# Expert weights of a routed layer: up weights tile by tile in a ring of three, down weights of all experts held on chip

## What is computed

```python
def _L0_ffn_ref(tgt, Wr, br, W1, b1, W2, b2, gamma, beta):
    B, S, D, F, E = (2, 512, 256, 1024, 8)
    ...
    logits = jnp.einsum('bsd,ed->bse', tgt, Wr) + br
    top_v, top_i = jax.lax.top_k(logits, 2)
    top_w = jax.nn.softmax(top_v, axis=-1)
    ...
    h = jnp.einsum('bsd,efd->bsef', tgt, W1) + b1
    h = jax.nn.relu(h)
    o = jnp.einsum('bsef,edf->bsed', h, W2) + b2
    tgt2 = jnp.einsum('bsed,bse->bsd', o, router_w)
    return _layer_norm(tgt + tgt2, gamma, beta)
```

## Time and profile before

| what | us |
|---|---|
| median of 3 runs | 1827.38 |
| lowest and highest of them | 1818.76, 1833.07 |
| the profiled execution, its own time | 1823.52 |
| span of the profile | 1821.8 |
| the expert loop, from the first load of `xs` to the last output on DVE | 1156.5 to 1449.9 |

### The profile page before, as it was taken

One profiled execution on the slowest core, in us unless ns is written; L12 is line 12 of the kernel. 1 busy time (PEld: TensorE's weight loads), 2 busy tenths in 40 slices (PEclk: granted clock), 3 DMA queues, 4 the chain that ended last, 5 costly groups with the idle time before them and its releaser, 6 DMA issues.

```text
span 1821.8 us, 44029 instructions
## 1 busy us (share of the span) xinstructions
PE 1562.2 (86%) x18034; PEld 1282.3 (70%) x18034; DVE 1237.7 (68%) x2503; ACT 705.7 (39%) x1312; POOL 898.0 (49%) x862
## 2 busy tenths in 40 slices
PE   1899999999998999999999973499989855898798
PEld 0677777787777777877787752488888743566587
DVE  8757777777777678777777765244478666555765
ACT  1434544454444444444444431244534514222122
POOL 3246555665563365566565651576555616221322
PEclk9999999999999999999999986799999965655699
DMA  9134433442432253335334301799999781700001
GB/s 215 37 72 114 105 83 94 106 117 75 102 93 63 69 123 77 95 94 127 90 85 106 102 36 54 289 407 406 402 385 397 267 156 12 116 3 1 35 12 35
DMA packets 92973, 239.39 MB, mean 131 GB/s; under 512 B 17611, under 2 KB 40707, under 8 KB 92388
## 3 DMA queue, kind: packets, MB, share of 16 engines
q1 hardware_dynamic: 89028, 226.32, 43.0%
q0 software_dynamic: 3744, 10.26, 1.5%
HBM read 144.31 MB, written 39.72 MB: 101 GB/s over the span
## 4 chain that ended last, share of the span: by engine, by line
PE 53%; DVE 15%; DMA 13%; POOL 8%; issue 5%; ACT 2%; SPq 0%; DVEq 0%; ACTq 0%; POOLq 0%
PE ps L1916 21%; PE ps L2015 9%; DMA xs<-xslots 8%; PE ps L1949 5%; PE ps L1995 5%; PE ps L1996 5%; DMA latf<-wexp 4%; POOL PR L864 3%; DVE PR L1415 3%; POOL wst L876 2%; PE ps L2182 2%; DVE mxs L1349 2%; PE ps L2274 2%; DMA QS<-NM 1%; DVE wtmp L1443 1%
## 5 line engine op out<-in xcount | busy, mean ns | idle before, releaser
L864 POOL TENSOR_TENSOR PR<-PT 128x512 f16<-128x512 f32 (+1 forms) x416 | 441.2, 1070 | 421.7 <-ACT PT L1088 421.0
L1088 ACT ACTIVATE PT<-ps 128x512 f32<-128x512 f32 (+1 forms) x576 | 323.8, 596 | 366.0 <-PE ps L1996 365.8
L2015 PE MATMUL ps<-V_h,PT 128*128 128x65 f16 (+1 forms) x2304 | 324.9, 197 | 26.5 <-DVE PR L1415 20.7
L2015 PE MATMUL ps<-V_l,PT 128*128 128x65 f16 (+1 forms) x2304 | 320.4, 195 | 0.0
L2015 PE MATMUL ps<-V_l,PR 128*128 128x65 f16 (+1 forms) x2304 | 318.7, 194 | 0.0
L2015 PE MATMUL ps<-V_h,PR 128*128 128x65 f16 (+1 forms) x2304 | 318.2, 194 | 0.0
L2015 PEld LDWEIGHTS ps<-V_h,PT 128*128 128x128 bf16 (+1 forms) x2304 | 226.9, 98 | 121.2 <-issue 48.6
L1349 DVE TENSOR_REDUCE mxs<-ps 128x1 f32<-128x736 f32 x256 | 235.3, 919 | 48.3 <-PE ps L1949 48.3
L1995 PE MATMUL ps<-QA,KA 128*128 128x512 f32 (+1 forms) x576 | 247.8, 430 | 5.8 <-DMA QB<-maxT 5.2
L1996 PE MATMUL ps<-QB,KB 65*128 65x512 f32 (+1 forms) x576 | 231.0, 401 | 0.0
L2015 PEld LDWEIGHTS ps<-V_l,PT 128*128 128x128 bf16 (+1 forms) x2304 | 228.9, 99 | 0.7
(11 more groups left out here) (351 smaller groups left out, 3645.6 us busy)
## 6 DMA issues: line engine op xcount, KB each, us to landing
wx<-wsplit SPq DMA_DIRECT2D x46, 2048.0 KB, 11.4
QA<-Q_h SPq DMA_DIRECT2D x64, 256.0 KB, 4.6
latf<-wexp SPq DMA_DIRECT2D x32, 512.0 KB, 4.3
wsplit<-wst SPq DMA_DIRECT2D x32, 512.0 KB, 2.9
KA<-K_h SPq DMA_DIRECT2D x32, 275.5 KB, 3.1
KA<-K_l SPq DMA_DIRECT2D x32, 275.5 KB, 4.0
KB<-K_h SPq DMA_DIRECT2D x32, 275.5 KB, 5.4
QB<-Q_l SPq DMA_DIRECT2D x32, 256.0 KB, 5.5
```

Source lines behind the costliest of these rows:

```text
L864: nc.gpsimd.tensor_tensor(PR[0:m, s % RING, :], PT[0:m, s % RING, :], upper(s)[0:m], ALU.subtract).then_inc(s_rem_pool, 1)
L1088: nc.scalar.activation(PT[0:m, s % RING, :], score_banks[s % 2][0:m], ACT.Exp, scale=HD ** -0.5).then_inc(s_exp, 1)
L2015: mm = nc.tensor.matmul(pv_bank[:, q, :], p, v, start=(kt == 0 and q == 0 and k == 0), stop=(kt == KT - 1 and k == 3), skip_group_check=True)
```

## The change

`wx`, a ring of four with the whole expert (64 KB in each partition), is gone. In its place are `wup`, a ring of three with the up weights of a tile (24 KB in each partition), and `wdn`, which holds the down weights of all eight experts (64 KB in each partition).

- SP issues eight transfers of 1 MB for `wdn` once the last piece of `wsplit` is stored (`s_wst`), before it waits for the sorted slots (`s_sorted`). In the loop it transfers 1 MB for each tile, after a wait for the up product of tile j-3.
- PE reads the expert number of each tile itself (`value_load` in `slot_turn`). Its down matmuls address `wdn` by a register.
- Before its first down product PE waits for all of `wdn`.

```diff
@@ in the SP program
             sp.wait_ge(s_wst, 16 * E0 * PIECES)
+            for e in range(E0):
+                sp.dma_start(wdn[:, e].rearrange("p s k n -> p s (k n)"),
+                             wsplit[e, NC:].rearrange("s p k n -> p s (k n)")).then_inc(s_wdn, 16)
             sp.wait_ge(s_sorted, 3)
 
             def load_weights(j):
                 e = nc.sync.value_load(etu[0:1, j:j + 1], min_val=0, max_val=E0 - 1)
                 if j >= WR:
-                    sp.wait_ge(s_down, j - WR + 1)
-                sp.dma_start(wx[:, j % WR].rearrange("p s k n -> p s (k n)"),
-                             wsplit[bass.ds(e, 1)].rearrange("o s p k n -> p (o s) (k n)")).then_inc(s_wx[j % WR], 16)
+                    sp.wait_ge(s_up, 2 * (j - WR + 1))
+                sp.dma_start(wup[:, j % WR].rearrange("p s k n -> p s (k n)"),
+                             wsplit[bass.ds(e, 1), 0:NC].rearrange("o s p k n -> p (o s) (k n)")).then_inc(s_wup[j % WR], 16)
@@ in the PE program
             def slot_turn(j):
+                experts[j] = nc.tensor.value_load(etu[0:1, j:j + 1], min_val=0, max_val=E0 - 1)
                 pe.wait_ge(s_xs[j % XS], 16 * (j // XS + 1))
...
+            def up_weights(j, c, part, cols):
+                return wup[:, j % WR, c, "hl".index(part), cols]
+
+            def down_weights(j, piece, part, cols):
+                return wdn[:, bass.ds(experts[j], 1), piece, "hl".index(part), cols].squeeze(1)
...
             def down(j):
+                if j == 0:
+                    pe.wait_ge(s_wdn, 16 * E0)
```

More of the change, by code:

```diff
@@ L58 @@
 XS = 3
-WR = 4
+WR = 3
 DS = 6
@@ L202, in program @@
         b2s = sb1("b2s", [P, E0, D])
-        wx = sb1("wx", [P, WR, PIECES, 2, PW], F16)
+        wup = sb1("wup", [P, WR, NC, 2, PW], F16)
+        wdn = sb1("wdn", [P, E0, PIECES - NC, 2, PW], F16)
         LT0 = sb1("LT0", [E0, GR, HALF])
@@ L337, in program @@
         s_scales = sem("scales_ready")
-        s_wx = [sem(f"tile_weights{r}_loaded") for r in range(WR)]
+        s_wup = [sem(f"tile_up_weights{r}_loaded") for r in range(WR)]
+        s_wdn = sem("down_weights_loaded")
         s_b1 = sem("expert_biases_loaded")
@@ L2157, in slot_turn @@
                 mm.then_inc(s_xt, 1)
-            def weights(j, piece, part, cols):
-                return wx[:, j % WR, piece, "hl".index(part), cols]
+            def up_weights(j, c, part, cols):
+                return wup[:, j % WR, c, "hl".index(part), cols]
+            def down_weights(j, piece, part, cols):
+                return wdn[:, bass.ds(experts[j], 1), piece, "hl".index(part), cols].squeeze(1)
             def up(j):
                 pe.wait_ge(s_xl, j + 1)
-                pe.wait_ge(s_wx[j % WR], 16 * (j // WR + 1))
+                pe.wait_ge(s_wup[j % WR], 16 * (j // WR + 1))
                 for f in range(FC):
@@ L2169, in up @@
                     mm = product(hidden_banks[n % 4][:, f % 4 * P:f % 4 * P + P],
-                                 [(weights(j, c, a, slice(f * P, f * P + P)), xsp[b][:, j % 2, c, :])
+                                 [(up_weights(j, c, a, slice(f * P, f * P + P)), xsp[b][:, j % 2, c, :])
                                   for c in range(NC) for a, b in RANDL])
@@ L2182, in down @@
                         mm = nc.tensor.matmul(out_banks[j % 2], hs[a][:, j % 2, f * P:f * P + P],
-                                              weights(j, NC + f // 4, b, slice(f % 4 * D, f % 4 * D + D)),
+                                              down_weights(j, f // 4, b, slice(f % 4 * D, f % 4 * D + D)),
                                               start=(f == 0 and i == 0), stop=(f == FC - 1 and i == 2))
```

## The result

The changed kernel takes 1810.45 us (median of 8 runs, 1808.67 to 1816.01), the kernel before 1827.1 us (median of 8, 1818.76 to 1835.01). The ratio is 0.991, with a 95% interval of 0.9886 to 0.9933: 0.9% faster, 16.65 us between the medians.

A forecast was written before the change was run, and what follows sets the result against it. Bytes bound the loop's first half, above a 5.5 us tile floor. Savings of 13.6, 1.5 and 3.0 us sum to 18.1, less 1 for register steps: 17 off 1827.4 gives 1810 us, range 1799 to 1836.

The forecast's parts named there:

- the start: Around the first tiles: with half the bytes ahead, tile 3's rows land earlier; 1.5 us saved, between 0 and 3.
- the register steps: PE's expert-number read and address steps in each tile mostly fit under its array work; 1 us cost for the loop.
- Bytes bound the first stretch: Loop's first half, 1170.4 to 1327.5: DMA engines always busy at 404 GB/s, so transfers set the 6.04 us a tile.
- Tiles 1 to 27: Early loop: 26 tiles go from 6.04 to the 5.52 us floor; 13.6 us saved.
- `og`: Tile 27 to 28: DVE's 4.57 us wait for expert outputs goes; 3.0 us saved, at most 4.6.
- Later tiles: Other tiles with extra DVE work, and the last ones from 1412 on, keep their pace; nothing saved.
- `wdn`: Eight down-weight loads before the loop hide behind the router; cost 0, up to 21 us without cover.
- The rule of the Trainium skill: PE's down product: firmware-handled matmuls cost about 62 ns each; if so, 0.1 to 0.5 us in each of 35 tiles.
- DMA share near 0.6: Sign expected in the loop of the profile after the change.
- the first two (read or queue on the path): PE: read exposed, 1825 (0.20, shared with transfers not binding); or queue becomes the bound, about 1860 (slower, 0.15).
- the third (a bigger gain): Early tiles at 5.48 us, full 4.6 us on expert outputs, 3 us at the start: 22 us saved, 1805; chance 0.10.
- the fourth (the transfers don't bind): Loop stays at 6 us, set by DVE, ACT and POOL: 1827; chance 0.20, shared with the exposed PE read.

The follow-up runs named there:

- experiments 2 and 3: 2: changed kernel, but all 2 MB transferred per tile, 1828.28 us; 3: kernel before, but only the 1 MB up half transferred, 1812.47 us.
- Experiment 4: Changed kernel, but the eight down-weight transfers issued only once the tokens are scattered, so nothing covers them; 1833.79 us, ratio 1.0038.
- experiment 1: Changed kernel, but PE reads no expert number and takes down weights from a fixed place (output wrong); 1807.45 us, ratio 0.9886.
- experiments 5 and 6: Changed kernel, but PE reads the expert number twice per tile, 1812.69 us, or four times, 1861.42 us.
- experiment 8: Changed kernel with DVE's extra output work cut into nine parts per group and its expert-number read moved ahead of the part; 1798.65 us, ratio 0.9848.

## Why the prediction was right

The forecast was 1810 us, measured are 1810.45. The mechanism held. That the numbers lie only 0.45 us apart is luck: the start was taken too large by 1.5 us and the register steps by 0.6, which cancel in part, and the runs of one kernel scatter by several us. By its own steps:

- **Bytes bound the first stretch.** Shown by experiments 2 and 3: the bytes put back alone take the whole gain away, the bytes halved alone give it.
- **Tiles 1 to 27: 13.6 us.** Measured 157.1 - 144.0 = 13.1. The floor was 5.54 us and not 5.52.
- **The start: 1.5 us, between 0 and 3.** This term is wrong, and the runs show nothing in its place: from the bias load `b2s` (1096.05 and 1101.58) to the first `hf` the kernels take 68.0 and 68.1 us (0.3 us less from the first load of `xs` on, 0.4 us more up to it), and tile 1 came 6.3 us after tile 0 in both. The wait that the term was read from comes behind the `hf` of tile 1 at 1170.40, so it lies within tiles 1 to 27 and was counted there already:

```profile
1173.38 0.44 PE L2156 MATMUL ps<-ident,xs 128*128 128x128 f32 x2 [1.00 <-DMA xs<-xslots]
```

  Without it tile 2 follows 5.48 us after tile 1 instead of 5.70, a part of the 13.1. Ahead of the transposes of tile 2 PE waited 0.53 us for rows in the kernel before and does not now, and nothing came of it: the `hf` of tile 1 hangs on something else. The first up product takes 4.97 us and not 2.68; PE had been idle for 30.6 us before the loop (granted clock 0.50 from 1166.7 to 1171.0, the level of 1.2 GHz, against 1.00 from 1171.5 on). From its end the chain goes through `hf`, ACT and `xsp_l` to the `hf` of tile 1, while the up product of tile 1 is done 1.4 us before that `hf`.
- **`og`: 3.0 us.** Measured 11.52 - 8.57 = 2.95; DVE's sum takes 5.06 us as in the second such tile. (The last two lines of the earlier trace rows, with its 8.55 us, are tiles 34 and 35, not 35 and 36.)
- **Later tiles: nothing.** Tiles 28 to 42 keep their 5.5 to 8.6 us.
- **`wdn`: 0.** The loads ended near 1128, 26 us after their first issue, where 22.5 to 27.5 were forecast; not by 1125, because this profile is 5.5 us late at that place. They were still 11 us early. Experiment 4 puts the price without cover at 23 us, where 21 was given.
- **Register steps: 1 us.** 0.4 us of the loop by experiment 1. The rows of ACT gave the right sizes (46 ns for a step, 0.3 and 0.15 us for a read), and the lead of PE's queue held, with less than one read to spare (experiments 5 and 6). The forecast sum took 0.43 us for a read; with the gaps between its pieces it takes 0.59.
- **The rule of the Trainium skill.** With a register in the address 16 steps and 24 matmuls passed the queue in about 2.1 us (first step at 1190.4, read at 1192.5), under the 2.62 us of the array, and in the kernel before 24 matmuls without steps took 1.6 us (1180.9 to 1182.5). By the Trainium skill, page "TensorE: Matmul & The Clock Gate", section "Wait — 56ns, not 53.3ns?", a matmul that goes through firmware costs the queue about 62 ns. No run here shows which way these are decoded; the case in which 0.1 to 0.5 us a tile comes through did not occur, since experiment 1 finds 0.4 us for all 46.
- **DMA share near 0.6.** It was 0.78 at 262 GB/s: 3.4 us of 5.5 would be 0.62, and 262 of 404 GB/s is 0.65, but the share of busy time was higher than the share of bytes. That step was a size off and carried no part of the sum.
- **The other signs.** How long `xs` takes to land could not be checked, since the view has no landing time for it; its transfers are no longer in the chain. Of the rivals, the first two (read or queue on the path) fall with experiment 1, the third (a bigger gain) with the 5.54 us a tile and the start, the fourth (the transfers don't bind) with experiments 2 and 3.

The loop's parts add up: 13.1 + 3.0 less 0.1 in the tiles behind them are the 15.9 us between the loops (285.8 and 269.9 us), against 16.65 between the medians. The rest, 0.7 us, is within the scatter of the runs. Which of the two floors, PE or the ring of DVE and ACT, sets the 5.5 us is not shown; no run moved one of them down alone.

## What to carry to other kernels

Before you cut transfers, look for the floor that stands under them: here 2.6 us of transfers were taken off each tile, and only 0.5 us of it came back as time, because PE and a ring of DVE and ACT were both at 5.5. A one-time load belongs where an idle stretch of the queue is long enough for all its bytes, and its price outside that stretch is about bytes over bandwidth (21 us estimated, 23.3 measured). Register steps on an engine are free as long as its queue runs ahead of its work; measure how far ahead it runs by when its waits are passed, and after the change look at which engine reads registers behind its own last result, as DVE did here.

## What the hardware showed that I had not expected

- A matmul whose operand address comes from a register was not slower than one with a fixed address: mean 273 ns in both, 2.62 us for 24 of them, with two register steps of 46 ns among every three.
- The DMA share says less than the GB/s. At 1.5 MB a tile the share was 1.00 with 354 GB/s and no tile was late; at 2 MB it was 1.03 with 406 GB/s and the tiles took 6.05 us on average instead of 5.54.
- Eight transfers of 1 MB in a row took SP 10.7 us to issue, 1.3 us each, where single ones took 0.4. In another place (experiment 4) the same eight took 7.0 us. Why is open.
- A wait that the view puts down to ACT (0.80 us) was mostly the reader's own: moving DVE's read of a number left 0.30 us (experiment 8).
